# One whole 1024-column scan per unit in place of two 512-column scans, with a seam step on ScalarE

## The reference

```python
deltaA = jnp.exp(delta[..., None] * A)
deltaBx = delta[..., None] * Bm[:, :, None, :] * xc[..., None]

def step(h, inp):
    dA, dBx, c = inp
    h = dA * h + dBx
    return (h, jnp.einsum('bdn,bn->bd', h, c))
```

## Time and profile before

| | |
|---|---|
| median of 3 runs | 5141.44 us (5140.6 to 5143.02) |
| span of the profiled execution | 5139.8 us |
| VectorE busy | 4789.5 us, 93% |
| TensorE busy | 4759.9 us, 93% |
| GpSimd busy | 3832.3 us, 75% |
| ScalarE busy | 3336.0 us, 65% |
| mean granted TensorE clock | 0.975 |

### The profile page before, as it was taken

One profiled execution on the slowest core, in us unless ns is written; L12 is line 12 of the kernel. 1 busy time (PEld: TensorE's weight loads), 2 busy tenths in 40 slices (PEclk: granted clock), 3 DMA queues, 4 the chain that ended last, 5 costly groups with the idle time before them and its releaser, 6 DMA issues. The chain is left out here.

```text
span 5139.8 us, 67238 instructions
## 1 busy us (share of the span) xinstructions
PE 4759.9 (93%) x21964; PEld 3283.1 (64%) x21964; DVE 4789.5 (93%) x5476; ACT 3336.0 (65%) x7037; POOL 3832.3 (75%) x1722
## 2 busy tenths in 40 slices
PE   8799899998999989999999898967999999999999
PEld 3555555555555555555555555555888888888888
DVE  8999999999999999999999999997888888888887
ACT  3777877777777787777777877765444444444442
POOL 6999999999999999999999999994322322322231
PEclk9899999999999999999999999988999999999999
DMA  7555565655656556566566666554010011001000
GB/s 268 173 198 194 189 204 185 196 195 191 199 188 200 195 186 204 186 198 196 188 199 188 194 199 191 187 172 156 25 38 31 31 34 35 31 31 37 31 31 29
DMA packets 402675, 745.79 MB, mean 145 GB/s; under 512 B 44083, under 2 KB 44211, under 8 KB 402198
## 3 DMA queue, kind: packets, MB, share of 16 engines
q1 hardware_dynamic: 401590, 738.08, 43.7%
q0 software_dynamic: 736, 3.41, 0.2%
HBM read 698.05 MB, written 43.26 MB: 144 GB/s over the span
## 5 line engine op out<-in xcount | busy, mean ns | idle before, releaser
L717 POOL TENSOR_TENSOR slot<-du,b_row 128x1024 f32<-128x1024 f32 x1024 | 2397.9, 2379 | 0.2
L1050 DVE TENSOR_TENSOR_SCAN decays<-decays,state,slot 128x512 f32<-128x512 f32 x1376 | 1686.6, 1270 | 61.6 <-POOL slot L717 50.3
L917 ACT ACTIVATE decays<-delta,rate 128x512 f32<-128x512 f32 x2048 | 1385.0, 687 | 50.6 <-DVE slot L998 2.2
L1111 PE MATMUL work_ps<-h_t,win 128*128 128x512 f32 x2048 | 981.8, 627 | 137.5 <-ACT delta L853 109.1
L1188 PEld LDWEIGHTS y_ps<-ident,slot 128*128 128x128 f32 x8192 | 946.2, 143 | 238.2 <-issue 177.9
L1188 PE MATMUL y_ps<-ident,slot 128*128 128x128 f32 x8192 | 1020.9, 277 | 42.6 <-POOL slot L724 30.7
L1574 POOL TENSOR_TENSOR hq<-hid,qinv 128x1408 f32<-128x1408 f32 x63 | 163.5, 2596 | 1001.7 <-DVE qinv L1600 1001.7
L1057 DVE TENSOR_TENSOR slot<-decays,c_row 128x512 f32<-128x512 f32 x1376 | 870.8, 673 | 0.0
L724 POOL TENSOR_TENSOR slot<-slot,c_row 128x1024 f32<-128x1024 f32 x336 | 797.7, 2374 | 81.8 <-ACT state L906 79.7
L1050 DVE TENSOR_TENSOR_SCAN slot<-decays,state,slot 128x512 f32<-128x512 f32 x672 | 819.0, 1263 | 4.0 <-POOL slot L717 2.2
L1111 PEld LDWEIGHTS work_ps<-h_t,win 128*128 128x128 f32 x2048 | 393.7, 201 | 590.0 <-issue 493.1
(11 more groups left out here) (274 smaller groups left out, 7356.9 us busy)
## 6 DMA issues: line engine op xcount, KB each, us to landing
b_row<-b_c_rows SPq DMA_DIRECT2D x1024, 256.0 KB, 3.9
c_row<-b_c_rows SPq DMA_DIRECT2D x1024, 256.0 KB, 3.8
win<-in_w_in SPq DMA_DIRECT2D x256, 256.0 KB, 4.4
xt<-in_x SPq DMA_DIRECT2D x16, 1024.0 KB, 7.1
xr<-in_x SPq DMA_DIRECT2D x64, 256.0 KB, 4.4
x_after_mamba<-xr SPq DMA_DIRECT2D x64, 256.0 KB, 4.6
xa<-x_after_mamba SPq DMA_DIRECT2D x64, 256.0 KB, 3.0
xres<-x_after_mamba SPq DMA_DIRECT2D x64, 256.0 KB, 2.7
```

What stands on the lines that cost most here:

```text
L717: pool.tensor_tensor(slot[:, u % SLOTS, :, :], du[:, p % 2, :, :], two(b_row[:, u % BC_RING, :]), ALU.mult).then_inc(S["ub_ready"], 1)
L917: act.activation(decay[u % 2][:, i, :], delta[:, p % 2, i, :], ACT.Exp, scale=rate[:, 2 * p + i, n:n + 1]).then_inc(S["decay_ready"], 1)
L1050: dve.tensor_tensor_scan(d if u in DVE_C else h, d, h, state[:, 2 * p + i, n:n + 1], ALU.mult, ALU.add).then_inc(S["scan_done"], 1)
L1111: op = pe.matmul(dst[:, :], win[:, i % WIN_RING, k, :], h_t[:, k, :], start=(k == 0), stop=(k == KT - 1))
```

## The change

For each pair the two rows of 512 columns are scanned as one row of 1024, with the state of block 2p as its start. At column 512 the second block begins, and there the recurrence must start from another state. Two things are done for that. `cut` sets the first `delta` of the second row to 1e30 after du has been made, so that the decay at the seam is 0. `seam`, one 128x1 activation on ScalarE for each unit, adds to the input at the seam what is missing there: the true first decay times the saved state of block 2p + 1. That product, `carry`, is made for 16 states at a time by GpSimd in `du_of`, from `first_decay`, one 128x16 exponential in `softplus`. The scan waits for `seam`, and `seam` waits for `times_b`.

The product on VectorE becomes one instruction of 1024 columns, and the save one copy of two columns, which waits for the whole product. `half_used` is gone. Units 1, 13 and 18 join `DVE_C`, now 46 units.

```diff
+CUT = 1e30
...
+    10: [("cut", 1, 0)], 16: [("softplus", 2, 0), ("xd", 2, 0)], ...
...
+    25: [("h_out", 1, 1), ("residual", 3, -1), ("cut", 2, 0)], ...
...
+    47: [("cut", 3, 0)], 48: [("in_out", 6, 1), ("xd", 7, 0)], ...
...
+    58: [("softplus", 0, 1)], 61: [("z_out", 1, 1)], 62: [("cut", 0, 1), ("xd", 1, 1), ("z_out", 2, 1)], ...
...
 DVE_C = (
-    2, 3, 4, 6, 8, 9, 11, 12, 14, 15, 16, 19, 20, 21, 22, ...
+    1, 2, 3, 4, 6, 8, 9, 11, 12, 13, 14, 15, 16, 18, 19, 20, 21, 22, ...
...
+            first_decay = sb("first_decay", [P, 2, N])
+            carry = sb("carry", [P, 2, N])
...
                         pool.tensor_tensor(du[:, p % 2, :, :], delta[:, p % 2, :, :], xc[c.parity][:, 2 * p:2 * p + 2, :],
                                            ALU.mult).then_inc(S["u_ready"], 1)
+                        wait(pool, S["first_ready"], c.at(PAIRS, p + 1))
+                        wait(pool, S["state_saved"], c.at(UNITS, N * (p + 1) - UNITS))
+                        wait(pool, S["seam_ready"], c.at(UNITS, N * (p - 1)))
+                        pool.tensor_tensor(carry[:, p % 2, :], first_decay[:, p % 2, :], state[:, 2 * p + 1, :],
+                                           ALU.mult).then_inc(S["carried"], 1)
...
                         act.preload_act_table_set("natural_log_exp_and_others")
+                        wait(act, *piece_read("d", 2 * p + 1, c))
+                        wait(act, S["carried"], c.at(PAIRS, p - 1))
+                        act.activation(first_decay[:, p % 2, :], rate[:, 2 * p + 1, :], ACT.Exp,
+                                       scale=delta[:, p % 2, 1, 0:1]).then_inc(S["first_ready"], 1)
+
+                    def cut(p, c):
+
+                        wait(act, S["first_ready"], c.at(PAIRS, p + 1))
+                        wait(act, S["u_ready"], c.at(PAIRS, p + 1))
+                        act.activation(delta[:, p % 2, 1, 0:1], one[:, :], ACT.Copy, scale=CUT).then_inc(S["cut_done"], 1)
...
-                    def save_state(u, i, c):
+                    def save_state(u, c):
                         p, n = divmod(u, N)
-                        if u in DVE_C:
-                            wait(act, *((S["half_used"], half_used(u, c)) if i == 0 else c_done(u, c)))
-                            act.activation(state[:, 2 * p + i, n:n + 1], decay[u % 2][:, i, T - 1:T], ACT.Copy).then_inc(S["state_saved"], 1)
...
+                        h = decay[u % 2] if u in DVE_C else slot[:, u % SLOTS, :, :]
+                        wait(act, *(c_done(u, c) if u in DVE_C else (S["scan_done"], c.at(UNITS, u + 1))))
+                        act.activation(state[:, 2 * p:2 * p + 2, n], h[:, :, T - 1], ACT.Copy).then_inc(S["state_saved"], 1)
...
+                            if i == 1:
+                                wait(act, S["cut_done"], c.at(PAIRS, p + 1))
+                        if exists(cc) and v in DVE_C and i == 0:
+                            wait(act, S["state_saved"], c.at(UNITS, u - 1))
...
+                    def seam(u, c):
+
+                        p, n = divmod(u, N)
+                        h = slot[:, u % SLOTS, 1, 0:1]
+                        if n == 0:
+                            wait(act, S["carried"], c.at(PAIRS, p + 1))
+                        wait(act, S["ub_ready"], c.at(UNITS, u + 1))
+                        act.activation(h, h, ACT.Identity, bias=carry[:, p % 2, n:n + 1]).then_inc(S["seam_ready"], 1)
...
-                            for i in range(2):
-                                if saving:
-                                    save_state(v, i, cc)
-                                if exists(c):
+                            if saving:
+                                save_state(v, cc)
+                            if exists(c):
+                                for i in range(2):
                                     decays(pos, i, c)
+                                seam(pos, c)
...
+                        wait(dve, S["decay_ready"], c.at(2 * UNITS, 2 * u + 2))
+                        wait(dve, S["seam_ready"], c.at(UNITS, u + 1))
+                        d = decay[u % 2].rearrange("p a t -> p (a t)")
+                        h = slot[:, u % SLOTS, :, :].rearrange("p a t -> p (a t)")
+                        dve.tensor_tensor_scan(d if u in DVE_C else h, d, h, state[:, 2 * p, n:n + 1],
                                                ALU.mult, ALU.add).then_inc(S["scan_done"], 1)
...
+                    def times_c(u, c):
+                        wait(dve, *ring_loaded(c_loaded, c, u))
+                        wait(dve, S["scan_done"], c.at(UNITS, u + 1))
+                        dve.tensor_tensor(slot[:, u % SLOTS, :, :], decay[u % 2], two(c_row[:, u % BC_RING, :]),
+                                          ALU.mult).then_inc(c_row_used[u % BC_RING], 1)
```

More of the change, by code:

```diff
@@ L519, in last_pieces @@
                 return {BANK[ka]: ka for ka in order}
-            def half_used(u, c):
-                return c.at(len(DVE_C), sum(v <= u for v in DVE_C))
             def c_done(u, c):
@@ L721, in times_c @@
                         h = slot[:, u % SLOTS, :, :]
-                        wait(pool, S["state_saved"], c.at(2 * UNITS, 2 * u + 2))
+                        wait(pool, S["state_saved"], c.at(UNITS, u + 1))
                         wait(pool, *ring_loaded(c_loaded, c, u))
@@ L1040, in _, with scan @@
                     HAVE = {"x_low": x_low, "gate": gate}
[L1042 removed]
+                    def scan(u, c):
                         p, n = divmod(u, N)
[L1044 to L1051 removed]
@@ L1053, in times_c @@
[L1053 to L1061 removed]
+                        if n == 0:
+                            wait(dve, S["state_saved"], c.at(UNITS, N * (p + 1) - UNITS))
@@ L1065, in body @@
                             if exists(c):
-                                scan(pos, 0, c)
-                                scan(pos, 1, c)
+                                scan(pos, c)
                             for step, arg, cc in steps(DVE_STEPS, c, (pos, 0)):
```

39 lines of the change are left out of this document (8 added, 31 removed).

## The result

| | before | after |
|---|---|---|
| median | 5141.0 us | 5326.1 us (5324.9 to 5327.8, 4 runs) |
| ratio | | 1.0359, 95% interval 1.0345 to 1.0374 |
| span of the profiled execution | 5139.8 us | 5323.1 us |
| one chunk | 212.4 us | 224.5 us |

The change costs 185 us. The forecast was 5218 us, in a range of 5090 to 5280: the sign was right, the size was less than half of what came, and the range missed it.

A forecast was written before the change was run, and what follows sets the result against it. VectorE was taken as the path, GpSimd close behind. Per chunk, 206.0 us of work, 10.7 of stops behind ScalarE and 0.5 for gates and slots gave 217.2 against 212.4: 5218 us, range 5090 to 5280.

The forecast's parts named there:

- That is 0.12 us for each of 46 units: VectorE: new wait of each product for the scan just before it, 0.12 us, in 46 units a chunk.
- 1024 take 2.24: VectorE: a scan of 1024 columns has an interval of 2.24 us, as one fixed part is saved.
- A product of 1024 takes 1.13: VectorE: one product of 1024 columns has an interval of 1.13 us, two halves before taking 0.59 each.
- The rival of no fixed cost saved: VectorE: a scan of 1024 still takes 2.36 us, work 7.7 us a chunk more; 5318 us, chance 0.04.
- The rival by the Trainium skill: VectorE: no wait between scan and product, a semaphore costing nothing extra; 5152 us, chance 0.04.
- The six stops, 10.7 us: VectorE stopped behind ScalarE's long steps (softplus, silus, conv and input pieces), with smaller places 10.7 us a chunk.
- The windows: ScalarE's time for other steps before VectorE needs its decays: 3.4 us after, up to 5.0 before; longer steps stop VectorE.
- The seam is done at E + 1.8, ScalarE is free at E + 1.7.: ScalarE: times after E, the end of the product two units back, with the seam at 284 ns; window 3.4 us.
- a seam waits for its slot and blocks ScalarE: ScalarE: one of two causes in the rival of 14 us of stops a chunk; 5271 us, chance 0.14.
- GpSimd's own waits for saved states ... stay.: GpSimd: its waits for saved states remain at 4.7 us a chunk, since the saves come later.
- Feedback (5271): Rival: late ScalarE delays TensorE and itself again, or a seam blocks it; 14 us of stops, 5271 us, chance 0.14.

The follow-up runs named there:

- e10: Changed kernel with the C row waited for ahead of the scan, its seam step neither reading nor awaiting the slot, old state not added: 5235.4 us.
- e1: Changed kernel with VectorE's wait for the C row moved from the product to ahead of the scan: 5292.9 us.
- e5: Changed kernel without seam step and carries, and with the C row waited for ahead of the scan: 5180.1 us.
- e13: Changed kernel with the two silu activations of a chunk cut from 4096 to 2048 columns: 5273.1 us.
- e4: Changed kernel with the products of units 1, 13 and 18 back on GpSimd, as in the kernel before: 5339.2 us.
- e12: Kernel before with the product of unit 1 on VectorE as well, 44 units: 5129.4 us.
- e11: Changed kernel without seam and carries, C row awaited ahead of the scan, third decay buffer in SBUF, saves three positions behind: 6051.9 us.

## Why the prediction was wrong

Its sign was right, and so was its picture: VectorE is the path, and ScalarE's long steps stop it. Two steps of the sum failed: "That is 0.12 us for each of 46 units", and the seam, priced at its duration and with nothing for its wait. By the chunk, the forecast was 217.2 us and 224.5 came, 7.3 more. VectorE's own work is 5.7 us of that (211.7 against 206.0), the stops 1.6 (12.8 against 10.7 + 0.5). By the runs, e10, which has the step's time but neither of the two costs left out, takes 5235 us against the forecast's 5218. The second wait is 33 us (after to e1), the seam held by its slot 58 us (e1 to e10). These are differences in a row from after to e10, so that they add up to 5326 shows nothing by itself; what each is comes from its edit.

- **"1024 take 2.24", "A product of 1024 takes 1.13".** Nearly right: the intervals are 2.26 and 1.14, durations 2346 and 1224 ns. The rival of no fixed cost saved is out; that its 5318 us lies nearest to the measured time is chance.
- **"That is 0.12 us for each of 46 units."** The first step that failed, and the larger one by the chunk. The earlier trace rows gave the price of one dependence; the product carries a second wait, and starts 0.10 us after the scan's end, not 0.03. VectorE's own work came to 211.3 us by the rows, 211.7 by the chunk less its stops, not 206.0: 3.2 us are this wait, some 2 the 0.01 to 0.02 us by which 64 scans and 46 products were priced low. e1 shows the wait: 33 us. The rival by the Trainium skill ("VectorE: DVE Perf Modes", "The DRAIN you can't avoid"), whose chain of eight copies takes the same time with a semaphore after each, is out by the same rows: 0.12 us from a start beside the one before to a start behind it, and 0.07 more for a second.
- **The six stops, 10.7 us.** The windows were right for what they counted. With a seam step that waits for nothing (e10) the stops at 4, 17, 22, 29 and 54 are within 0.2 us of the forecast; those forecast at 40 and 59 (1.1 and 0.5) were 0.5 and nothing, so the sum is 9.7. Without the step (e5) it is 6.4. e13 shows the rule at the two silus.
- **"The seam is done at E + 1.8, ScalarE is free at E + 1.7."** The second step that failed. It takes the seam at its 284 ns and leaves its wait for the slot at nothing, without a reason. Measured, ScalarE stands 147.6 us in all before seams for GpSimd's slots, and where a long step follows (positions 3, 16 and 53) VectorE stops longer: 13.4 us a chunk against 9.7 where the step does not wait, 3.7 us. Before, only VectorE waited for slots, and it could not delay a silu; now the wait is on the engine whose lead is already short. The prediction named this, "a seam waits for its slot and blocks ScalarE", as a half sentence in a rival of 0.14, and priced it with the feedback at 3.3 us of stops, nearly that; but forecast and rival should have been one case, since nothing in the trace of before spoke against it: GpSimd worked 98% of the stage and VectorE already waited 41.2 us for its slots.
- **"GpSimd's own waits for saved states ... stay."** They did not: 4.7 to 19.6 us a chunk. But this is not by itself a cost. In e5, where no seam waits for a slot, they are still 150.6 us in the same 2800, 11.6 a chunk; GpSimd has time to wait when the others are slower. It matters only where the next slot is then late for the seam.
- **The range.** It ended at 5280, just above that rival. Feedback (5271) together with 0.07 us more for each product (51 us, less what stops give back) leads to 5304 to 5322; no case combined two costs. That the stops came out near the forecast in sum (12.8 against 11.2) is partly luck: 3.7 us left out stand against 1.5 us too much elsewhere, and 0.6 us that VectorE's longer work hides.

What is only argued: the loop from late save to late slot to held seam. No run cut it at the save alone, and the waits do not all rise and fall together: in the same 2800 us of e4 the seam waits 154.8 us and VectorE 177.7 for it (111.0 and 145.3 after), while GpSimd waits 206.8 us for saved states (245.3 after), since it has more work. Where the 17 us between 5218 and e10 lie is told only by the chunk (218.5 against 217.2): 208.8 us of own work against 206.0, and 9.7 of stops against 11.2.

## What to carry to other kernels

A tiny step put on an idle engine is priced by where it stands and what it waits for, not by its duration: 0.28 us 64 times on ScalarE cost 113 us, half of it because the step lies in the window in which ScalarE must catch up after a long step, half because it moved a wait for GpSimd onto that engine. Merging instructions makes the next one dependent on the last: count for each what waits it carries and what ran between, since 64 scan starts saved were eaten by 46 dependent products (VectorE's own work was 208.5 us a chunk before, 208.6 with one wait in e5, 211.7 with two). And where two engines are both at 98%, moving the one product that balances them (e12, 11 us gained) was worth more than this rewrite of both.

## What was unexpected of the hardware

- On VectorE the product starts 0.034 us after the end of the scan that it needs with one wait, and 0.104 us after with two (medians of e1 and after, 33 us in all), though the wait for the row of C held up no scan when it stood there. The two waits in the other order were not tried.
- VectorE's scan and product with both inputs in SBUF took 3566 and 2857 ns in the mean beside GpSimd, against 2344 and 1224 with one input in PSUM, and GpSimd's products went from 2362 to 2881 ns (e11). Where GpSimd stood idle, the same scan and product took 2337 and 1225 ns: it is the two engines together that cost.
